# State-space chunks: the sums of y's squares, GpSimd's three sums and one product against eight products on TensorE

## The reference

```python
h = layernorm(h)
z, xBC, dt = split(h @ in_w.T)              # 1024, 1024 + 2*32, 32 columns
dt  = softplus(dt + dt_bias)
xBC = silu(causal_conv(xBC, taps=4) + conv_b)
x, B, C = split(xBC)                        # 32 heads of 32, B and C of 32 states
state_t = exp(dt*A)*state + (dt*x_t) B_t ;  y_t = C_t . state_t + D*x_t
y = y * silu(z)
y = y * rsqrt(mean(y*y, -1) + 1e-5) * rms_w # the sum of squares over 1024 channels
h = h + y @ out_w.T
```

## Time and profile before

| | |
|---|---|
| median of 3 runs | 1617.61 us (1614.58 to 1622.73) |
| the profiled execution | 1618.92 us, its span 1617.4 us |
| mean granted clock of TensorE | 0.893 of full speed |
| PE busy | 1297.6 us, 80% |
| DVE busy | 1079.4 us, 67% |
| ACT busy | 747.7 us, 46% |
| POOL busy | 341.7 us, 21% |
| L903, the three sums on POOL | 48 instructions, 39.5 us |
| L1006, the one product on PE | 32 passes, 4.5 us with latency |

### The profile page before, as it was taken

One profiled execution on the slowest core, in us unless ns is written; L12 is line 12 of the kernel. 1 busy time (PEld: TensorE's weight loads), 2 busy tenths in 40 slices (PEclk: granted clock), 3 DMA queues, 4 the chain that ended last, 5 costly groups with the idle time before them and its releaser, 6 DMA issues.

```text
span 1617.4 us, 34487 instructions
## 1 busy us (share of the span) xinstructions
PE 1297.6 (80%) x12750; PEld 899.7 (56%) x12751; DVE 1079.4 (67%) x1659; ACT 747.7 (46%) x1123; POOL 341.7 (21%) x365
## 2 busy tenths in 40 slices
PE   3735699988368999965569999756999999999991
PEld 2215576765266766723245555354677777776770
DVE  3676778887658888867876676563646774477333
ACT  2238466464556466422452323242556664466330
POOL 0112334534313534520220000014000000000004
PEclk9757799999689999987779999955999999999996
DMA  8133000000310000014120000036425663354005
GB/s 289 39 145 108 9 3 2 1 1 2 137 34 4 2 1 2 1 52 157 63 79 1 0 0 0 0 121 260 169 104 214 233 228 128 130 197 162 26 26 162
DMA packets 35639, 133.10 MB, mean 82 GB/s; under 512 B 8120, under 2 KB 9912, under 8 KB 25600
## 3 DMA queue, kind: packets, MB, share of 16 engines
q1 hardware_dynamic: 27424, 104.04, 17.7%
q0 software_dynamic: 8160, 28.32, 5.2%
HBM read 109.67 MB, written 22.68 MB: 82 GB/s over the span
## 4 chain that ended last, share of the span: by engine, by line
PE 48%; DVE 22%; issue 12%; ACT 6%; POOL 6%; DMA 5%; DVEq 0%; POOLq 0%; SPq 0%; ACTq 0%
PE banks L2133 14%; PE banks L2154 14%; DVE mb_ca L607 6%; PE banks L1665 4%; PE banks L1695 3%; PE banks L975 2%; PE banks L999 2%; POOL mb_ysq L903 1%; POOL xs_table L2166 1%; POOL mb_ring L926 1%; POOL mb_quad L931 1%; DMA eb_un<-ys_table,eb_slot 1%; DVE mb_S L676 1%; PE banks L340 1%; PE banks L1068 1%
## 5 line engine op out<-in xcount | busy, mean ns | idle before, releaser
L2133 PE MATMUL banks<-eb_x_hi,eb_w_hi 128*128 128x128 f16 x1344 | 228.9, 220 | 2.1 <-DVE eb_x_lo L2033 2.1
L2133 PE MATMUL banks<-eb_x_lo,eb_w_hi 128*128 128x128 f16 x1344 | 228.8, 220 | 0.0
L2133 PE MATMUL banks<-eb_x_hi,eb_w_lo 128*128 128x128 f16 x1344 | 228.8, 220 | 0.0
L975 PE MATMUL banks<-mb_u_hi,mb_wi_hi 128*128 (+3 forms) x1152 | 203.8, 222 | 29.7 <-ACT mb_sz L830 15.5
L975 PE MATMUL banks<-mb_u_hi,mb_wi_lo 128*128 (+3 forms) x1152 | 203.2, 221 | 0.0
L975 PE MATMUL banks<-mb_u_lo,mb_wi_hi 128*128 (+3 forms) x1152 | 203.1, 221 | 0.0
L607 DVE SCALAR_TENSOR_TENSOR mb_ca<-mb_xp,mb_par,mb_ca 128x128 f32<-128x128 f32 x384 | 159.1, 477 | 6.0 <-ACT mb_ca L799 4.0
L975 PEld LDWEIGHTS banks<-mb_u_hi,mb_wi_hi 128*128 128x128 f16 (+1 forms) x1152 | 113.9, 99 | 47.6 <-issue 46.2
L2133 PEld LDWEIGHTS banks<-eb_x_hi,eb_w_hi 128*128 128x128 f16 x1344 | 132.5, 99 | 4.8 <-issue 2.5
L2133 PEld LDWEIGHTS banks<-eb_x_lo,eb_w_hi 128*128 128x128 f16 x1344 | 132.5, 99 | 2.4
L2133 PEld LDWEIGHTS banks<-eb_x_hi,eb_w_lo 128*128 128x128 f16 x1344 | 132.5, 99 | 0.0
(11 more groups left out here) (433 smaller groups left out, 3113.6 us busy)
## 6 DMA issues: line engine op xcount, KB each, us to landing
eb_raw<-e_w SPq DMA_DIRECT2D x36, 1024.0 KB, 5.4
eb_un<-e_w SPq DMA_DIRECT2D x28, 1024.0 KB, 7.7
mb_ring<-m_in_w SPq DMA_DIRECT2D x8, 1072.0 KB, 6.0
xs_table<-zero POOLq DMA_DIRECT2D x1, 6400.0 KB, 20.7
eb_xg<-xs_table POOLq DMA_DIRECT2D x23, 256.0 KB, 2.9
ys_table<-eb_y POOLq DMA_DIRECT2D x21, 256.0 KB, 6.5
ab_raw<-a_in_w SPq DMA_DIRECT2D x4, 1154.0 KB, 12.3
mb_ring<-m_out_w SPq DMA_DIRECT2D x4, 1024.0 KB, 5.2
```

Source lines behind the costliest of these rows:

```text
L975: x = e.matmul(ps[0:width, bank, n * P:(n + 1) * P], a[:, k, f:f + width], b[:, k, ds(i * P, P)], start=(k == 0 and m == 0), stop=(k == KD ...
L2133: o = e.matmul(ps[:, j, c * P:(c + 1) * P], a[:, side, k, f * P:(f + 1) * P], b[:, k, :], start=(k == 0 and m == 0), stop=(k == KD - 1 and ...
```

## The change

The three sums and their semaphore go. PE waits for the squares themselves and adds up eight products, one for each group of channels, in PSUM. The parts of the B/C convolution get tiles of their own, as `ysq` is now read longer. On POOL `dx` (L931) follows the faded state (L926) with no sums between them, and a wait for POOL's own `yi + dx` of the chunk before is set ahead of it.

```diff
+    part = [sb(f"part{k}", [NS, 2, P])[:] for k in range(TAPS - 1)]
...
-    acc_bc, ysum_done = sem("acc_bc"), sem("ysum_done")
+    acc_bc = sem("acc_bc")
...
-                part = [ysq[0:NS, 2 * k + 2:2 * k + 4, :] for k in range(TAPS - 1)]
...
-            def sum_squares(g):
-
-                e.wait_ge(ysq_done, g + 1)
-                for k, half in enumerate((4, 2, 1)):
-                    e.tensor_tensor(ysq[:, 0:half, :], ysq[:, 0:half, :], ysq[:, half:2 * half, :], ALU.add)\
-                        .then_inc(ysum_done, 1)
-                    e.wait_ge(ysum_done, 3 * g + (k + 1))
...
                 e.tensor_tensor(heads(faded), heads(S[:]), edec[0:NS, i, :].unsqueeze(2).to_broadcast([NS, H2, 32]),
                                 ALU.mult).then_inc(smul, 1)
+                e.wait_ge(xc_done, 2 * (g + 1))
                 if not is_first:
-                    sum_squares(g - 1)
-                e.wait_ge(xc_done, 2 * (g + 1))
+                    e.wait_ge(yid_done, g)
                 e.tensor_tensor(dx, xc[:], par[:, MB_DCOL:MB_DCOL + JD].unsqueeze(2).to_broadcast([P, JD, P]), ALU.mult)\
                     .then_inc(dx_done, 1)
...
             chunks(e, l, body)
-            sum_squares(l * TT + TT - 1)
             power(l * TT + TT - 1)
...
             def sum_rows(g):
 
-                e.wait_ge(ysum_done, 3 * g + 3)
-                e.matmul(ps[:, 2, 384:385], ysq[:, 0, :], core.ones[:, 0:1], start=True, stop=True).then_inc(rms_mm, 1)
+                e.wait_ge(ysq_done, g + 1)
+                for j in range(JD):
+                    x = e.matmul(ps[:, 2, 384:385], ysq[:, j, :], core.ones[:, 0:1], start=(j == 0), stop=(j == JD - 1))
+                x.then_inc(rms_mm, 1)
```

## The result

| | before | after |
|---|---|---|
| median | 1616.32 us | 1675.71 us (1674.34 to 1675.90, 4 runs) |
| span of the profiled execution | 1617.4 us | 1674.0 us |
| mean granted clock | 0.893 | 0.879 |

The ratio is 1.0358 (95% interval 1.0328 to 1.0388): the change makes the kernel slower by 59 us, where 70 were forecast. The two profiled executions are 56.7 us apart, as the one before was 2.6 us longer than its median.

A forecast was written before the change was run, and what follows sets the result against it. The prediction took a loop through PE and DVE, without POOL, to set the chunk's length; 24.0 + 26.2 + 20 = 70 us gave 1688 us, 4.3% slower, with eight in ten runs from 1638 to 1706.

The forecast's parts named there:

- The row sum: PE's L1006: 14 added f32 passes at 0.107 us, 1.50 us a chunk, 16 times, 24.0 us in all.
- The upper bound of 0.136 from the transposes: PE's L1036 at full clock, 128 columns each: 0.136 us a pass, so at most 1.90 us a chunk for the added passes.
- POOL's work was off the path: POOL's three sums L903, 2.62 us a chunk, had time to spare on both sides, so removing them gives nothing.
- The rival that took the page's chain at its word: POOL's sums are on the path: 14 chunks regain 39 us against 24 paid, 1603 us, faster; chance 0.04.
- The handover: At the end of L926 POOL's L931 goes before DVE's waiting L696, delaying it 1.87 us in 14 chunks, 26.2 us.
- The rival by the Trainium skill: DVE's L696, issued first, goes before POOL's L931; only PE's passes remain, 1642 us; chance 0.30.
- The clock: PE's idle stretch before L975 grows to 3.27 us; falls to 1.2 GHz cost 2.0 us in 10 of 14 chunks, 20 us.

## Why the prediction was right, point by point

- **The row sum.** Forecast 1.50 us a chunk at 0.107 a pass; it is 1.56 at 0.112 a pass. The rows of the router at half the clock carried over. The upper bound of 0.136 from the transposes held their latency: their starts are 0.109 apart, close to what was measured. Of the 16 row sums 15 count: at the end of the second layer DVE has other work up to L617 and L618 and waits 0.0 us for the sum in both kernels, where the prediction had it wait. The Trainium skill ("TensorE: Matmul & The Clock Gate", section on weight-path perf modes) has it that fp32 weights get no fast load; eight f16 products in 0.21 us against 1.70 for the f32 ones agree with that.
- **POOL's work was off the path.** L903 is gone and nothing came back. The rival that took the page's chain at its word is out: DVE's wait for the row sum went up by 1.56 us.
- **The handover.** Forecast: L931 wins, 1.87 us in each of 14 chunks. It is 1.86. The experiments with `dx` held back and with a gap take it away, and the move alone brings it back. The rival by the Trainium skill ("SBUF — State Buffer", section "Who interferes with whom"), that issue order decides, is refuted here: the gate was issued 0.90 us ahead of `dx` and waited for the whole of it. With two instructions of 128 partitions the rule's outcome did hold. With DVE's turn won, the time was 1652 to 1653 us and not the 1642 of that rival, as it had no falls behind the row sum.
- **The clock.** This is the term that was mis-sized: 20 us forecast for ten falls of 2.0 us behind an idle stretch of 3.27. It is 3.26 us in 3 of the 12 steady chunks, each time with a fall at its end, at 1.1 to 1.2 us, 3.4 in all; in the others at most 1.82 of it is left. What I missed is that the clock falls behind the row of one-column passes too, 1.6 to 3.0 us after its end, in 9 of the 12. After such a fall PE reaches its transposes 4.00 us behind the new state instead of 2.51 (267.02 less 263.02, and 299.14 less 296.63), and so fills the idle stretch from the front. In the last chunk of each layer the same fall costs: it is 6.5 us longer, not 3.4, and the window from 424.0 us shows PE busy throughout at 1.2 GHz, DVE for 2.30 us of 6.50 and ACT for 0.08; 6 us for both layers. That it is this fall alone is argued from the window, not tested. Less the 1.3 by which chunk 0 to 1 had been long before, and with 0.6 more between the layers, this makes some 9 us instead of 20.
- **The sum.** 15 x 1.56 = 23.4, 14 x 1.86 = 26.0 and 9 make 58.4 us, for the measured 58.3 from the first new state to the last. That the medians differ by 59.4 is in part chance: the stretch up to the first new state alone varies by 2.7 us between executions (195.4 to 198.1).

That the parts don't add is shown by the experiments: by the medians the products alone (`dx` held back) cost 36 us, the move alone 42, both together 59; from the first to the last new state it is 35, 37 and 58.

## What to carry to other kernels

Before an instruction is taken from POOL, look at what slides up into its place: here it slid beside an instruction of DVE's with two SBUF inputs that is on the path, and a wait for POOL's own last instruction, 0.17 us, gave DVE the turn. Price a product with few columns by the load of its weights, and put such products between wide ones. Where two changes both touch TensorE's clock, run each alone: their sum says little of both. And look at the stages that were not edited: some 6 us came or went there.

## What was not expected of the hardware

- Between POOL and DVE, with no gap between POOL's instructions, the waiting DVE instruction got its turn after one of 128 partitions (L697 2.03 us) and not after one of 32 followed by one of 128 (3.88 us); in the kernel before it did after one of 32 followed by another of 32. Why is open. No run shows what POOL does in between.
- 16 one-column passes in 1.84 us were followed by a fall to 1.2 GHz 1.6 to 3.0 us later in 9 of the 12 steady chunks, and in all 12 (0.8 to 2.9 us later) in each of the three versions with these products in a row and the gate at 2.02 us, with PE busy all the time in the windows shown; the same passes between wide products were followed by none in the steady chunks.
- The same fourth stage took 248.7 or 254.3 us from its first to its last product, the first where its clock had two low stretches of 3.4 us and the second where it had five.
